# Expert down-projection as three fp32r products with hi/lo hidden activations, and linear attention on centred v, in a five-stage software pipeline

## The reference

```python
# A: linear attention, 8 heads of 16, with rope on q and k
kv = einsum('bshd,bshe->bhde', k, v); ksum = k.sum(1); vsum = v.sum(1)
num = einsum('bshd,bhde->bshe', q, kv) * scale + vsum[:, None]
den = einsum('bshd,bhd->bsh', q, ksum) * scale + seq_len
o = (num / den[..., None] + lepe_conv(v)) * (x @ Wg.T)
x = layernorm(x + o @ Wo.T)
# B: dense product plus a top-1 low-rank expert (ranks 1, 2, 4, 8)
x = layernorm(x + x @ W.T + low_rank_expert(x))
# C: causal attention with one head of 128
x = layernorm(x + softmax_causal(q @ k.T) @ v)
# D: 16 experts of width 64, top 4 by groups, and a shared expert of width 128
g = silu(einsum('th,efh->tef', x, w1_e)); u = einsum('th,efh->tef', x, w3_e)
routed = einsum('tef,ehf,te->th', g * u, w2_e, combine)
x = layernorm(x + routed + swiglu(x, w1_s, w3_s, w2_s))
```

## Time and profile before

| | |
|---|---|
| time, median of 3 (lowest to highest) | 746.12 us (743.97 to 746.69) |
| profiled execution: its own time | 746.4 us |
| its span, first to last instruction | 744.6 us |
| PE busy | 683.6 us, 92% |
| DVE busy | 591.7 us, 79% |
| ACT busy | 445.6 us, 60% |
| POOL busy | 403.9 us, 54% |
| granted TensorE clock, mean | 0.96 |

### The profile page before, as it was taken

The page is one execution under the profiler, slowest core; times in us unless marked ns, Lnnn a source line. Parts: engine busy times, 40 slices in busy tenths (PEclk is TensorE's granted clock), DMA queues, the critical chain, the costliest instruction groups (busy, mean ns, idle before and its releaser), DMA issues.

```text
span 744.6 us, 13318 instructions
## 1 busy us (share of the span) xinstructions
PE 683.6 (92%) x3798; PEld 531.5 (71%) x3798; DVE 591.7 (79%) x1855; ACT 445.6 (60%) x850; POOL 403.9 (54%) x857
## 2 busy tenths in 40 slices
...
DMA packets 18677, 12.50 MB, mean 17 GB/s; under 512 B 704, under 2 KB 18240, under 8 KB 18368
## 3 DMA queue, kind: packets, MB, share of 16 engines
...
## 4 chain that ended last, share of the span: by engine, by line
PE 39%; POOL 27%; issue 23%; DVE 6%; ACT 2%; POOLq 1%; DMA 1%; SPq 0%; DVEq 0%; ACTq 0%
POOL moment L1154 8%; PE bank L556 7%; POOL rstd L1154 5%; PE bank L356 4%; PE bank L347 4%; PE bank L349 4%; PE bank L348 4%; POOL qk L1134 3%; POOL centered L1199 2%; POOL x0T_lo L1184 2%; PE bank L469 1%; POOL x3T_lo L1189 1%; POOL x_b L1179 1%; POOL x L1193 1%; POOL x L1195 1%
## 5 line engine op out<-in xcount | busy, mean ns | idle before, releaser
L347 PE MATMUL bank<-x3T_hi,w_hi 128*128 128x512 f32 x288 | 146.8, 510 | 4.5 <-DVE gu L1044 4.5
L556 PE MATMUL bank<-hid,whole 128*128 128x512 f32 x288 | 147.9, 595 | 1.0 <-DVE hid L1047 1.0
L730 ACT ACTIVATE silu<-bank 128x512 f32<-128x512 f32 x144 | 85.6, 595 | 70.0 <-PE bank L349 68.3
L349 PE MATMUL bank<-x3T_hi,w_lo 128*128 128x512 f32 x288 | 113.7, 395 | 0.0
L348 PE MATMUL bank<-x3T_lo,w_hi 128*128 128x512 f32 x288 | 113.5, 394 | 0.0
L1044 DVE TENSOR_TENSOR gu<-silu,bank 128x512 f32<-128x512 f32 x128 | 87.3, 682 | 24.3 <-PE bank L349 22.0
L1054 DVE TENSOR_TENSOR hid<-gu,bank 128x512 f32<-128x512 f32 x128 | 87.5, 684 | 2.1 <-DVE gu L1044 0.2
L1141 POOL TENSOR_TENSOR rden_x<-rden,whole 128x512 f32<-128x512 f32 x16 | 17.4, 1086 | 128.6 <-DVE rden L844 128.6
L1154 POOL TENSOR_TENSOR moment<-stats 128x4 f32<-128x4 f32 x192 | 41.3, 247 | 84.3 <-DVE stats L860 84.3
L1134 POOL TENSOR_TENSOR qk<-rope_c,rope_s 128x512 f32<-128x512 f32 x32 | 40.5, 1278 | 71.3 <-DVE rope_s L831 71.3
L347 PEld LDWEIGHTS bank<-x3T_hi,w_hi 128*128 128x128 f32 x288 | 54.4, 189 | 31.2 <-issue 13.6
...
## 6 DMA issues: line engine op xcount, KB each, us to landing
...
```

The costliest lines, as they stand in the source:

```text
L347: mm(out, wh, mh, start=True, stop=False)
L349: return mm(out, wl, mh, start=False, stop=True)
L556: mm(YB[:], whole[:, a:a + P], hid[:, c % 2], start=c == 0, stop=c == CHUNKS).then_inc(p_w2.sem, 1)
L730: fn(silu[:, c % 2], GB[:], ACT.Silu).then_inc(a_silu.sem, 1)
```

## The change

The experts' down-projection becomes three fp32r products. For that w2 is split once into `w2_hi` and `w2_lo`, and `hid` is split for each chunk: `d_hi` on ACT copies it to fp32r (`hid_hi`), and `d_lo` on POOL subtracts (`hid_lo`). `d_down(c)` now waits for `hid_lo` of its chunk, `d_hi(c)` and `d_lo(c)` wait for the down product of chunk c-2, and `d_hid(c)` waits for `d_lo(c-2)`.

In stage A, v is made transposed by three fp32r products (`a_vT_`), ACT takes each sequence's mean off it (`neg_mean`, `v_cent`), PE transposes the centred v (`a_v_`), and kv is made with 8 columns of ones behind v, so that one product per tile gives numerators and denominators together (136 columns). The mean of v is added back behind the division (since num/den = mean + centred num/den). The division is done by DVE before the transposes (`a_att`), so `rden_x` goes; `a_mix` moves from POOL to DVE and `a_gate` from DVE to POOL. Two small additions of stage B are merged. w1, w3 and w2 are loaded to staging tensors, whose memory is taken over by `w2_hi`, `w2_lo`, `hid_hi` and `yT`; that puts waits into `split_late` in turn 1.

```diff
 N_WEIGHT = _place(WEIGHT_COLS, ...)
-W_LATE, W_SPLIT = WEIGHT_COLS["w3"][1], WEIGHT_COLS["g"][1]
+W_LATE, W_SPLIT = WEIGHT_COLS["w3"][1], WEIGHT_COLS["v"][1]
...
+        with ExitStack() as early:
+            w_stage = early.enter_context(nc.sbuf_tensor("w_stage", [P, W_LATE], F32))
+            w2_stage = early.enter_context(nc.sbuf_tensor("w2_stage", [P, ALLCH * P], F32))
+        w2_hi = sb("w2_hi", [P, ALLCH * P], F32R)
+        w2_lo = sb("w2_lo", [P, ALLCH * P], F32R)
+        hid_hi = sb("hid_hi", [P, 2, BLOCK], F32R)
...
@@ TensorE @@
-            def a_v_(n):
-                pe.wait_ge(a_xT[0].sem, a_xT[0].at(n))
+            def a_vT_(n):
+                pe.wait_ge(g_x0l.sem, g_x0l.at(n))
                 if started(n):
                     pe.wait_ge(v_res[0].sem, v_res[0].at(n - 1))
-                for t in range(TILES):
-                    last = mm(tile(A1, t), tile(xT[0], t), raw("v"), start=True, stop=True)
-                last.then_inc(p_v.sem, 1)
+                mm3(A1[:], hi("v"), lo("v"), x0T_hi[:], x0T_lo[:]).then_inc(p_vT.sem, 1)
...
-            def a_vT_(n):
-                pe.wait_ge(a_v.sem, a_v.at(n))
+            def a_v_(n):
+                pe.wait_ge(a_cent.sem, a_cent.at(n))
                 pe.wait_ge(v_rope.sem, v_rope.at(n))
-                transpose_tiles(A1, lambda t: v_one[:, t, 0:P], ident).then_inc(p_vT.sem, 1)
+                transpose_tiles(A1, lambda t: tile(v_cent, t), ident).then_inc(p_v.sem, 1)
...
-            def a_den(n):
+            def a_num_(n):
                 pe.wait_ge(a_qT.sem, a_qT.at(n))
                 pe.wait_ge(v_kv.sem, v_kv.at(n))
-                for t in range(TILES):
-                    last = mm(A1[:, t * HEADS:(t + 1) * HEADS], tile(qT, t), ks_m[:, t // 2, :], start=True, stop=True)
-                last.then_inc(p_den.sem, 1)
-
-            def a_num_(n):
-                for s in range(SEQS):
-                    last = mm(A0[:, s * SEQ:(s + 1) * SEQ], kv_m[:, s, :], qT[:, s * SEQ:(s + 1) * SEQ], start=True, stop=True)
-                last.then_inc(p_num.sem, 1)
-
-            def a_rd(n):
-                pe.wait_ge(g_rd.sem, g_rd.at(n))
-                transpose_tiles(A1, lambda t: rden_x[:, t], ident).then_inc(p_rd.sem, 1)
+                for s, b in ((0, A0), (1, A1)):
+                    for i in range(2):
+                        last = mm(b[:, i * SEQ:i * SEQ + KV], tile(qT, 2 * s + i), kv_m[:, s, :], start=True, stop=True)
+                    last.then_inc(p_num.sem, 1)
+
+            def a_aT(n):
+                pe.wait_ge(v_att.sem, v_att.at(n))
+                transpose_tiles(A0, lambda t: att[:, t], ident).then_inc(p_aT.sem, 1)
...
             def d_down(n, c):
-                if c < CHUNKS:
-                    pe.wait_ge(v_hid.sem, v_hid.at(n, c + 1))
-                else:
-                    pe.wait_ge(v_gu.sem, v_gu.at(n))
+                pe.wait_ge(g_hidl.sem, g_hidl.at(n, c + 1))
                 if c == 0 and started(n):
                     pe.wait_ge(v_res[3].sem, v_res[3].at(n - 1))
-                a = CONST_COLS["w2"][0] + c * P
-                mm(YB[:], whole[:, a:a + P], hid[:, c % 2], start=c == 0, stop=c == CHUNKS).then_inc(p_w2.sem, 1)
+                wh, wl = tile(w2_hi, c), tile(w2_lo, c)
+                mm(YB[:], wh, hid_hi[:, c % 2], start=c == 0, stop=False)
+                mm(YB[:], wh, hid_lo[:, c % 2], start=False, stop=False)
+                mm(YB[:], wl, hid_hi[:, c % 2], start=False, stop=c == CHUNKS).then_inc(p_w2.sem, 1)
@@ ScalarE @@
+                act.wait_ge(setup_v.sem, 12 + 4)
+                fn(w2_hi[:], w2_stage[:], ACT.Copy).then_inc(setup_a.sem, 1)
...
+                fn(neg_mean[:], v_sum[:], ACT.Copy, scale=-1.0 / SEQ).then_inc(a_mean.sem, 1)
+                act.wait_ge(a_mean.sem, a_mean.at(n))
+                for s in range(SEQS):
+                    fn(v_cent[:, s * SEQ:(s + 1) * SEQ], vT[:, s, 2:2 + SEQ], ACT.Identity,
+                       bias=neg_mean[:, s:s + 1]).then_inc(a_cent.sem, 1)
...
+            def d_hi(n, c):
...
+                if c > 1 or started(n):
+                    act.wait_ge(p_w2.sem, p_w2.at(n, max(c - 1, 0)))
+                fn(hid_hi[:, c % 2], hid[:, c % 2], ACT.Copy).then_inc(a_hidh.sem, 1)
@@ VectorE @@
             def a_att(n):
-                dve.wait_ge(p_rd.sem, p_rd.at(n))
-                dve.wait_ge(a_num.sem, a_num.at(n))
-                tt(attT[:], numT[:], A1[:], ALU.mult).then_inc(v_att.sem, 1)
-
-            def a_gate(n):
-                dve.wait_ge(g_mix.sem, g_mix.at(n))
-                dve.wait_ge(a_g.sem, a_g.at(n))
-                tt(oT[:], mixT[:], gT[:], ALU.mult).then_inc(v_oT.sem, 1)
+                dve.wait_ge(v_rden.sem, v_rden.at(n))
+                for s, b in ((0, A0), (1, A1)):
+                    each = rden[:, 2 * s:2 * s + 2].unsqueeze(3).broadcast_to([P, 2, HEADS, HD])
+                    tt(att[:, 2 * s:2 * s + 2].rearrange("p t (h d) -> p t h d", d=HD),
+                       by_tile(b)[:, :, 0:P].rearrange("p t (h d) -> p t h d", d=HD), each, ALU.mult).then_inc(v_att.sem, 1)
+
+            def a_mix(n):
+                dve.wait_ge(p_aT.sem, p_aT.at(n))
+                dve.wait_ge(a_mean.sem, a_mean.at(n))
+                dve.wait_ge(v_conv.sem, v_conv.at(n))
+                for s in range(SEQS):
+                    stt(mixT[:, s * SEQ:(s + 1) * SEQ], A0[:, s * SEQ:(s + 1) * SEQ], neg_mean[:, s:s + 1], conv[:, s],
+                        ALU.subtract, ALU.add).then_inc(v_mix.sem, 1)
...
             def d_hid(n, c):
...
-                    dve.wait_ge(p_w2.sem, p_w2.at(n, max(c - 1, 0)))
+                    dve.wait_ge(g_hidl.sem, g_hidl.at(n, max(c - 1, 0)))
@@ GpSimd @@
-            def a_rd(n):
...
-                tt(rden_x[:].rearrange("p t (h d) -> p (t h) d", d=HD), heads, ones, ALU.mult).then_inc(g_rd.sem, 1)
...
+            def d_lo(n, c):
+                pool.wait_ge(a_hidh.sem, a_hidh.at(n, c + 1))
+                if c > 1 or started(n):
+                    pool.wait_ge(p_w2.sem, p_w2.at(n, max(c - 1, 0)))
+                tt(hid_lo[:, c % 2], hid[:, c % 2], hid_hi[:, c % 2].bitcast(F32), ALU.subtract).then_inc(g_hidl.sem, 1)
```

More of the change, by code:

```diff
@@ L45 @@
 UNITS = P // EXPERTS
+KV = P + HEADS
+LOGITS = PROJ + len(RANKS)
 ALLCH = CHUNKS + 1
```

287 lines of the change are left out of this document (152 added, 135 removed).

## The result

| | before | after |
|---|---|---|
| time, median of 4 runs (lowest to highest) | 745.58 us (743.97 to 746.69) | 821.97 us (820.33 to 822.82) |
| ratio, 95% interval | | 1.1027 (1.1009 to 1.1045) |

The change makes the kernel 10% slower. The forecast was 769 us, with 788 as the upper end; the sign was right and the size was not.

A forecast was written before the change was run, and what follows sets the result against it. PE's queue was taken to bound the full turns: 38.5 us of work plus 3.7 of waits, 42.85 with the loop's branch against 41.55. Over 13 turns +17, ramp +3, run-out +3 on 746.4 gave 769 us, range 728 to 788.

The forecast's parts named there:

- PE's work, 38.5 us a turn: PE's own work in a full turn, forecast to fall by 2.4, from 40.9 to 38.5 us.
- Three make 0.69: 0.17 less for each of 9 chunks: Down-projection on PE: three fp32r products at 0.69 us against one float32 at 0.86, saving 1.5 us a turn.
- (a): PE ahead of hidden 5, waiting for silu 4 behind the router's exponential on ACT: 1.3 us a turn.
- (c): PE's gate product waits 0.6 us for ACT's x3 copies, then 0.2 behind ACT's load, exp and low-rank copy.
- (d): PE's x3 transposes wait for POOL's b_norm, ln_of(2) and norm: 0.4 us, 0 to 1.
- Wait (b): PE's v product waits for POOL's x0T_lo, behind the d_lo of chunks 7 and 8: 0.7 us, 0 to 1.5.
- Wait (e): PE's small waits (copies of prob, x2 behind hi 6, division ahead of the transposes): 0.5 us together, 0 to 0.8.
- DVE loses two full-width products and gets as many columns in four shorter instructions: about 36, as before: DVE's busy time in a turn, forecast to stay at about 36 us.
- Rival B: POOL becomes the bound, with d_lo stretched x 1.35 by contention with DVE: turn 44.5 us, 791 us in all; chance 0.10.
- Run-out, +3: Turn 18, experts alone: longer chain behind hid and two buffers add 3 us, 0 to 5.
- Ramp +3: First turns: later split of w2 and v product ahead of q and k add 3 us, 0 to 6.
- Rival A: Waits are covered, staying at their low bound of 0.8 us: turn 39.95, 731 us in all; chance 0.23.

The follow-up runs named there:

- e1: Kernel after without POOL's nine hid_lo subtractions a turn, hid_hi read in place of hid_lo (low part missing from the result): 772.2 us, ratio 1.038.
- e3: Kernel after, its order and new attention kept, with the float32 down product and four buffers of hid: 777.4 us, ratio 1.045.
- e14: e1 with seven memsets of spare tiles added to DVE in each turn, POOL's load that of e1: 817.6 us, ratio 1.098.
- e2: Kernel after with POOL's nine subtractions a turn run unused on constants, hid_hi read in place of hid_lo: 817.3 us, ratio 1.099.

## Why the prediction was wrong

**PE's work, 38.5 us a turn: off by 1.1.** After's turn less its waits is 44.7 - 5.1 = 39.6, e1's 41.86 - 2.2 nearly the same, and e3's 42.67 - 2.2 = 40.5. So the down form (e3 to e1) gives 0.8 to 0.9 and not 1.5, and the attention (from 40.9 to 40.5) 0.4 and not 0.9. The step "Three make 0.69: 0.17 less for each of 9 chunks" is the larger miss, 0.09 a chunk. Behind a float32 piece the first fp32r product takes 0.31, not 0.23, from start to start, and in the turn shown five of the nine triples start so.

**Waits (a), (c) and (d): right.** Forecast 1.3, 0.6 with 0.2, and 0.4; measured 1.3, 0.6 with none, and 0.4.

**Wait (b): the number by luck.** Forecast 0.7, measured 0.9. But its cause was to be lo 7 and lo 8 ahead of `x0T_lo`, "10.6" us of POOL's work. In after POOL stands idle for 1.88 us between the bias and `x0T_lo`, waiting for DVE's `stats`, and e14 has the same wait without any `d_lo`.

**Wait (e), "small ones", 0.5: mis-sized.** `comb` and `oT` are 1.9 together. They are DVE's lateness: in e1 both are gone, in e14 both are back.

**"DVE loses two full-width products and gets as many columns in four shorter instructions: about 36, as before": the step that failed.** It has 41.7. The columns were right, the durations weren't: they were taken to be the same beside a POOL that works 35.8 us a turn and not 25. The runs show in its place a DVE that is held until POOL's instruction ends: 45 us of time with nothing waiting for POOL (e2 less e1), and the same 45 from DVE's lengthening alone (e14 less e1).

**The nearness to e1 is luck in part.** 42.85 us a turn and 769 us were forecast, and e1, without that hold, has 510.1 / 12 = 42.5 and 772. But its plain turns of 41.86 are 39.6 of work and 2.2 of waits, where the forecast's 42.2 was 38.5 and 3.7: two errors that cancel.

**Rival B had the right pair of engines and the wrong victim.** "If `d_lo` is stretched so (x 1.35)": `d_lo` took 1.29 (mean of 144), and DVE's small instructions were stretched by up to 0.9 us in the mean. I looked for the contention in POOL's rows and not in DVE's, where the kernel before shows it already: `lg` takes 0.17 us, but 1.00 and 0.67 in the two turns in which POOL's x3 was running, one in the ramp and one in the run-out. The spread of `centered` fits the same hold seen from the other side: it took 1.40 us where DVE's `comb` (two SBUF inputs) had started 0.19 ahead of it, 1.58 where 0.01 ahead, and 1.04 in the four turns without `comb`.

**Run-out, +3: mis-sized.** Behind the last transposes e1 has 145.7 us, 5.9 over before, of which a turn's growth is 1; e2 has 157.1, so the hold costs 11 us there too. Ramp +3: 4.9.

**Rival A** was out of reach: its waits at the low bound, 0.8, were 2.2 even without `hid_lo`.
